# Expert down products taken in pairs in a fused attention and mixture-of-experts kernel: both heads, then all 48-row tails

## The reference

```
scores = softmax(x @ gate_w.T); topk_w, topk_idx = top_k(scores, 6); topk_w /= sum(topk_w)
buf[e, slot] = x[token]                     # at most C = 384 tokens per expert
g = buf @ w_gate[e].T; u = buf @ w_up[e].T  # 256 -> 176
eo = (silu(g) * u) @ w_down[e].T            # 176 -> 256
y[token] += eo[e, slot] * topk_w
return y + shared_swiglu(x)
```

## Time and profile before

| what | us |
|---|---|
| median of 3 runs | 542.45 (541.57 to 545.41) |
| span of the profiled execution | 581.2 |
| PE busy in it | 528.9 (91%) |
| DVE, ACT, POOL busy | 348.5, 301.3, 334.4 |

### The profile page before, as it was taken

How to read it: one execution, slowest core, us unless ns; L and a number is a source line. 1 busy time by engine, 2 the same in 40 slices (tenths; PEclk the granted TensorE clock), 3 DMA queues, 4 the chain that set the end, 5 groups by cost and what they waited for, 6 DMA issues and landing times.

```text
span 581.2 us, 13626 instructions
## 1 busy us (share of the span) xinstructions
PE 528.9 (91%) x4267; PEld 446.2 (77%) x4267; DVE 348.5 (60%) x1107; ACT 301.3 (52%) x899; POOL 334.4 (58%) x365
## 2 busy tenths in 40 slices
PE   8799998988989894969999999999988999999991
PEld 7698988888889883858877878787766787778681
DVE  4968877777777874756554555555454555455512
ACT  3797777778777863311234444455544444445410
POOL 4482254555444546575146766766666676678840
PEclk9898998889777976899999999999999999999997
DMA  9999997722222222122999999999989999977556
GB/s 292 388 373 394 404 390 280 228 84 84 73 74 74 83 74 88 57 98 78 321 267 300 252 245 230 236 244 251 251 217 231 241 238 233 231 143 115 73 116 140
DMA packets 65857, 119.01 MB, mean 205 GB/s; under 512 B 11216, under 2 KB 43280, under 8 KB 62704
## 3 DMA queue, kind: packets, MB, share of 16 engines
q0 software_dynamic: 24576, 56.39, 37.0%
q1 hardware_dynamic: 39584, 58.75, 33.2%
q10 hardware_dynamic: 1616, 2.90, 1.4%
HBM read 57.28 MB, written 60.23 MB: 202 GB/s over the span
## 4 chain that ended last, share of the span: by engine, by line
PE 75%; DVE 7%; issue 4%; another core or an unknown queue 4%; ACT 4%; POOL 2%; DMA 1%; ACTq 0%; DVEq 0%
PE PS L958 17%; PE PS L976 9%; PE PS L962 7%; PE PS L979 7%; PE PS L629 4%; PE PS L945 4%; PE PS L696 4%; PE PS L809 3%; PE PS L767 3%; PE PS L609 3%; PE PS L784 2%; PE PS L713 2%; PE PS L795 2%; PE PS L719 2%
## 5 line engine op out<-in xcount | busy, mean ns | idle before, releaser
L1836 POOL DMA_INDIRECT expert_rows<-XR,slot x96 | 95.1, 990 | 86.9 <-PE PS L629 58.7
L1859 POOL DMA_INDIRECT out<-YE,dest x64 | 93.6, 1462 | 45.2 <-issue 24.7
L1859 POOL DMA_INDIRECT acc_b<-YE,dest x64 | 93.7, 1465 | 37.4 <-issue 14.0
L1234 ACT ACTIVATE YE<-PS,wsel 104x256 f32<-104x256 f32 (+14 forms) x128 | 53.4, 467 | 96.5 <-PE PS L979 78.1
L1061 ACT ACTIVATE SMX<-SMX,smax 128x112 f32<-128x112 f32 x256 | 75.0, 392 | 0.2 <-DVE smax L1464 0.2
L1649 DVE TENSOR_TENSOR HE<-SL,PS 128x216 f32<-128x216 f32 (+12 forms) x64 | 23.2, 362 | 52.0 <-ACT SL L1221 39.5
L1070 ACT COPY PT<-PS 112x512 f32<-112x512 f32 x64 | 36.0, 595 | 21.0 <-remote 15.8
L767 PE MATMUL PS<-VW,PT 112*64 112x17 f32 x960 | 35.8, 213 | 11.2 <-issue 11.2
L1640 DVE COPY XET<-PS 128x432 f32<-128x432 f32 (+12 forms) x64 | 36.5, 572 | 15.6 <-PE PS L945 11.4
L1626 DVE SCALAR_TENSOR_TENSOR hit<-XG,by_rank 112x12 f32<-112x12 f32 (+3 forms) x64 | 14.6, 229 | 49.3 <-DMA out<-YE,dest 33.7
L767 PEld LDWEIGHTS PS<-VW,PT 112*64 112x64 f32 x960 | 32.6, 140 | 14.8 <-issue 12.7
(11 more groups left out here) (236 smaller groups left out, 1146.0 us busy)
## 6 DMA issues: line engine op xcount, KB each, us to landing
expert_rows<-zero POOLq DMA_DIRECT2D x24, 1088.0 KB, 14.0
W<-in_w SPq DMA_DIRECT2D x24, 368.0 KB
XG<-expert_rows SPq DMA_DIRECT2D x24, 238.0 KB
XB<-in_w SPq DMA_DIRECT2D x15, 368.0 KB
SMX<-in_w SPq DMA_DIRECT2D x15, 368.0 KB
XG<-expert_rows SPq DMA_DIRECT2D x24, 204.0 KB
W<-in_w SPq DMA_DIRECT2D x24, 128.0 KB
XG<-expert_rows SPq DMA_DIRECT2D x10, 272.0 KB
```

Of the source, the lines that this page charges most:

```text
L1234: act.mul(YE[0:h, e.slot, t, :], PS[0:h, 5 + t, e.odd * D:(e.odd + 1) * D], wsel[0:h, e.slot, t:t + 1]).then_inc(y_ready, 1)
L1836: pool.indirect_dma_start(rows, bass.IndirectOffsetOnAxis(ap=slot[:, d2 % UN, k:k + 1], axis=0), XR[:, d2 % UN, :], None, bounds_check=EX ...
L1859: pool.indirect_dma_start(target, bass.IndirectOffsetOnAxis(ap=dest[0:h, e.slot, t:t + 1], axis=0), YE[0:h, e.slot, t, :], None, bounds_ch ...
```

## The change

PE takes the downs of experts e and e + 1 together, when e + 1 has been reached: both heads, then both tails, into the two halves of the same PSUM banks (only the first head opens the bank). Hidden products go one expert further ahead (e + 2) and turned rows two further (e + 4). HE gets four slots, in the space of the attention's PT; YE six (YS), with six semaphores; wsel and dest twelve (AHEAD). SP issues weights 10 experts ahead of the rows' counter instead of 12, after the rows of p + 4.

```
...
+YS = 6
...
-        wsel = sb("wsel", [P, UN, 2])
+        wsel = sb("wsel", [P, AHEAD, 2])
...
-        dest = sb("dest", [P, UN, 2], I32)
+        dest = sb("dest", [P, AHEAD, 2], I32)
...
-        HE = sb("HE", [P, 2, 2, MAIN])
-        YE = sb("YE", [P, UN, 2, D])
+        HE = PT[:, :, :, :].rearrange("p g j q -> p (g j q)").rearrange("p (u t n) -> p u t n", u=UN, t=2)
+        YE = sb("YE", [P, YS, 2, D])
...
# SP
                     expert_rows(expert(n), n % UN, 0, 2, HALF[n])
                     if p < 2:
                         weights(expert(AHEAD - 2 + p), AHEAD - 2 + p)
-                    if p + AHEAD < EX:
-                        sp.wait_ge(dn_done, p + 1)
-                        weights(expert(p + AHEAD), p % AHEAD)
+                    elif p - 2 + AHEAD < EX:
+                        sp.wait_ge(dn_done, p - 1)
+                        weights(expert(p - 2 + AHEAD), (p - 2) % AHEAD)
...
# PE
+                def down_head(e, opens):
+                    j, h = home(e), half(e)
+                    c = slice(e.odd * D, (e.odd + 1) * D)
+                    for t in range(nt):
+                        pe.matmul(PS[0:h, 5 + t, c], HE[:, e.slot, 0, t * h:(t + 1) * h], W2S[j][:, 0, :],
+                                  start=opens, stop=False)
+                def down_tail(e, closes):
+                    j, h = home(e), half(e)
+                    c = slice(e.odd * D, (e.odd + 1) * D)
+                    for t in range(nt):
+                        r = slice(64 * t, 64 * t + FT)
+                        mm = pe.matmul(PS[0:h, 5 + t, c], HE[r, e.slot, 1, t * h:(t + 1) * h], W2S[j][r, 1, :],
+                                       start=False, stop=closes)
+                    mm.then_inc(dn_done, 1)
...
+                def down_two(e):
+                    pe.wait_ge(h_ready, e.times(2, 4))
+                    pe.wait_ge(w2_doubled, e.times(1, 2))
+                    if not e.first():
+                        pe.wait_ge(y_ready, sums_before(e, nt))
+                    down_head(e, True)
+                    down_head(e + 1, False)
+                    down_tail(e, False)
+                    down_tail(e + 1, True)
...
+                def step(e):
+                    if has(e + 2, end):
+                        hidden(e + 2)
+                    if has(e + 4, end):
+                        rows_t(e + 4)
+                    if e.odd:
+                        down_two(e - 1)
...
                 hidden(Step(0))
+                rows_t(Step(2))
                 pe.wait_ge(sh_add, NT - NTL)
+                hidden(Step(1))
+                rows_t(Step(3))
                 in_flight(pe, step, half is even_half)
...
# ACT
-                    act.wait_ge(dn_done, e.times(1, 1))
+                    act.wait_ge(dn_done, e.times(1, 2 - e.odd if nt == 2 else 1))
...
+                def step(e):
+                    if has(e + 2, end):
+                        silus(e + 2)
+                        doubled(e + 2)
+                    if e.odd:
+                        weighted(e - 1)
+                        weighted(e)
...
# DVE
-                    if not e.first(UN):
-                        dve.wait_ge(y_stored[j], adds_before(e, nt))
+                    if nt == 1:
+                        dve.wait_ge(y_stored[y_home(e)], adds_before(e, nt))
+                    elif not e.first(AHEAD):
+                        dve.wait_ge(y_stored[y_home(e)], e.turn(32, -32, YS))
...
-                    if not e.first(2):
-                        dve.wait_ge(dn_done, e.times(1, -1))
+                    if not e.first(UN):
+                        dve.wait_ge(dn_done, e.times(1, 1 - UN))
...
+                lead = nt
+                def ahead(e):
+                    if has(e, end):
+                        product(e)
+                    if has(e + lead, end):
+                        rows_t(e + lead)
+                    if has(e, end):
+                        tail_products(e)
+                        choices(e)
                 def step(e):
+                    ahead(e + nt)
...
# POOL
+                pool.memset(YE[:, UN:YS, :, :], 0.0)
...
-                    hold(pool, y_stored[before.slot], before.turn(32, 32))
+                    hold(pool, y_stored[y_home(before)], before.turn(32, 32, YS))
...
```

More of the change, by code:

```diff
@@ L418, in home, with y_home, y_uses @@
             return e.off % AHEAD
+        def y_home(e):
+            return e.off % YS
+        def y_uses(j, end=EX):
+            return (end - 1 - j) // YS + 1
         def adds_before(e, nt):
-            return e.turn(32) if nt == 2 else e.turn(16, 16 * EX // UN)
+            return e.turn(32, 0, YS) if nt == 2 else e.turn(16, 16 * y_uses(y_home(e)), YS)
         def sums_before(e, nt):
@@ L525, in _ @@
                         weights(expert(AHEAD - 2 + p), AHEAD - 2 + p)
-                    if p + AHEAD < EX:
-                        sp.wait_ge(dn_done, p + 1)
-                        weights(expert(p + AHEAD), p % AHEAD)
+                    elif p - 2 + AHEAD < EX:
+                        sp.wait_ge(dn_done, p - 1)
+                        weights(expert(p - 2 + AHEAD), (p - 2) % AHEAD)
             with sp.Else():
[L530 to L539, removed]
+                for p in range(2):
                     sp.wait_ge(et_done, p + 1)
@@ L542, in _ @@
                     expert_rows(expert(p + UN), p % UN, 0, 2)
-                    if p + AHEAD < EX:
-                        sp.wait_ge(dn_done, p + 1)
-                        weights(expert(p + AHEAD), p % AHEAD)
+                    weights(expert(AHEAD - 2 + p), AHEAD - 2 + p)
+                with sp.Fori(0, EX // AHEAD - 1) as i:
+                    for j in range(AHEAD):
+                        hold(sp, et_done, i * AHEAD + (j + 3))
+                        hold(sp, idx_ready, i * AHEAD + (j + 3))
+                        expert_rows(expert(i * AHEAD + (j + 2 + UN)), (j + 2) % UN, 0, 2)
+                        hold(sp, dn_done, i * AHEAD + (j + 1))
+                        weights(expert(i * AHEAD + (j + AHEAD)), j)
+                for p in range(EX - EX % AHEAD - AHEAD + 2, EX - UN):
+                    sp.wait_ge(et_done, p + 1)
+                    sp.wait_ge(idx_ready, p + 1)
+                    expert_rows(expert(p + UN), p % UN, 0, 2)
+                    if p - 2 + AHEAD < EX:
+                        sp.wait_ge(dn_done, p - 1)
+                        weights(expert(p - 2 + AHEAD), (p - 2) % AHEAD)
                 def rest(p, j):
@@ L964, in hidden, with step_one @@
                     mm.then_inc(gt_done, 1)
+                def down_head(e, opens):
[12 more added lines that the diff above has]
+                    mm.then_inc(dn_done, 1)
                 def down(e):
[L967 removed]
                     pe.wait_ge(h_ready, e.times(2, 2))
[L970 to L971 removed]
+                    pe.wait_ge(y_ready, sums_before(e, nt))
+                    down_head(e, True)
+                    down_tail(e, True)
+                def down_two(e):
+                    pe.wait_ge(h_ready, e.times(2, 4))
+                    pe.wait_ge(w2_doubled, e.times(1, 2))
                     if not e.first():
                         pe.wait_ge(y_ready, sums_before(e, nt))
[L974 to L983, removed]
+                    down_head(e, True)
+                    down_head(e + 1, False)
+                    down_tail(e, False)
+                    down_tail(e + 1, True)
+                def step_one(e):
                     if has(e + 1, end):
@@ L1246, in step @@
                     weighted(e)
-                    if nt == 2 and has(e + 2, end):
+                def step(e):
+                    if has(e + 2, end):
+                        silus(e + 2)
                         doubled(e + 2)
+                    if e.odd:
+                        weighted(e - 1)
+                        weighted(e)
                 if nt == 1:
                     silus(Step(EX))
-                    rest_in_flight(act, step)
+                    rest_in_flight(act, step_one)
                     return
@@ L1256, in experts @@
                 silus(Step(0))
+                silus(Step(1))
                 in_flight(act, step, half is even_half)
@@ L1677, in experts @@
                 product(first)
-                tail_products(first)
                 if nt == 1:
+                    tail_products(first)
                     rest_in_flight(dve, step)
                 else:
+                    rows_t(first + 2)
+                    tail_products(first)
+                    ahead(first + 1)
                     in_flight(dve, step, half is even_half)
@@ L1881, in rest @@
                 before = e - 1
-                hold(pool, y_stored[before.slot], before.turn(16, 16 * EX // UN + 16))
+                hold(pool, y_stored[y_home(before)], before.turn(16, 16 * y_uses(y_home(before)) + 16, YS))
                 added(e, acc_b, 1, P)
@@ L1889, in landed @@
             def landed(nt):
```

(5 more changed lines are left out.)

39 lines of the change are left out of this document (16 added, 23 removed).

## The result

Over four runs each, the changed kernel took 594.18 us (590.2 to 597.58) and the kernel before 543.93 (541.57 to 545.53): a ratio of 1.092, interval 1.086 to 1.098. It is slower by 50 us. The forecast was 568, the upper end of its range 592.

A forecast was written before the change was run, and what follows sets the result against it. PE's own work bound the kernel before; late odd rows on SP's queue would then set 9.1 us per pair. 26 turns, start, last pairs and adds add 27 us, 608 against 581.2, scaled to 568 us; range 544 to 592.

The forecast's parts named there:

- a loop through SP's queue and the odd rows: SP asks for odd rows only after the pair's wait and three weight issues, so PE waits; 555 to 583 us, 60%.
- The saving by pairs: On PE, one of two passages into and out of the down tails goes: 0.37 us per pair, 11.8 us over 32.
- the first rival: Rows are in time at L945 of odd experts and PE gains: loop 199.4 us, time 533 us, chance 10%.
- The pair's turn of 9.1 us: 0.32 + 2.22 + 3.2 landing + 0.3 restart + 0.3 turning + 2.77 down, at every size; 26 turns make 236.6 us.
- the lone rows: The last rows, issued alone at 536.29, had all 112 packets moved in 2.3 us; the lower bound for landing.
- an upper 4.35: Upper bound for the odd rows' landing after L477, with 544 KB of weights ahead of them in SP's queue, none moved.
- The start, the last pairs, the end: First pair start B at 305.9 from hidden 0 at 287.55; last pairs 34.1 us; last adds 3.1 us more.
- The ratio 608.2 / 581.2: Forecast span over the profiled span of before, 1.046, carried over to the median run of 542.45: 568 us.
- the adds' loop at 8.6 us per pair: Adds to `out`: expert e waits until e - 2 has landed, a turn of 8.6 us that no ring shortens.
- the second rival: Short landing, nothing moves: rows land in 2.3 us, a pair takes 8.2; 546 us, chance 17%.
- The weights clog the queue: Third rival: rows land at the upper 4.35 us behind the weights, a pair takes 10.25; 598 us, chance 13%.
- The rings: Longer rings ease DVE's and ACT's waits; they return at most PE's 5.8 us of idle in the loop.

The follow-up runs named there:

- second profile of before: The kernel before, unchanged, run again for another profile; run time 542.14 us, span 540.4.
- xg6: The changed kernel with six buffers for gathered rows instead of four, silu's tile moved into the dead query tile; 547.24 us, ratio 1.011.
- thin: The changed kernel, loading only 64 columns of each part of the weights issued between the even and odd rank's rows; 589.46 us, ratio 1.086.
- rings_only: The kernel before with only the longer rings (six YE slots, twelve of wsel and dest), no pairs or new order; 542.2 us, ratio 1.001.

## Why the prediction was right and wrong

**Which way, and by what: right.** The kernel became slower by a loop through SP's queue and the odd rows, the bound that the forecast put at 60%. The chain above is its sum written out by the profile. Its signs are all there: PE idle before L957 once in two experts (mostly 0.5 to 1.5 us at 108 rows and more, 1.8 to 2.2 at 84); pairs of 9.0 to 9.9 at full clock, but for one of 10.55 whose rows took 4.6 from issue to use, with no trend from 128 rows (9.03) to the smallest experts (9.12); L486 at 2.6 us behind the pair's first product; a gap of 0.36 on each side of eight tails; DVE's waits for adds gone (39.8 us in the second profile of before); DMA share 0.84.

**The saving by pairs: right.** 0.37 per pair was forecast. Three pairs at 96 rows without late rows took 7.56, 7.56 and 7.54, where two experts before took 7.90: 0.35. With rows in time (`xg6`) the middle took 199.5; the first rival had worked out 199.4.

**The pair's turn of 9.1 us: the step that failed.** Its terms at full clock, over the 19 pairs that waited: rows issued at 2.73 (2.54 forecast), from issue to turning 3.52 (3.5: 3.2 landing and 0.3 restart), turning 0.39 (0.3), down 2.87 (2.77): 9.51. Each is a little long, and the disputed one, the landing, came out right. That was luck in part: 3.2 was chosen between the lone rows' 2.3 and an upper 4.35 that counted the bytes ahead in full, and `thin` gives the 436 KB of them that it leaves out at most 0.6. With the first pair, 20 pairs took 189.7 in all: 7.7 us over the forecast. The six others took 11.26, 2.16 more than forecast: 13.0 us. There the mis-sized term is the paired down, 4.48 instead of 2.77, because the durations of PE's work in the turn came from 300 to 420 us of before, where PE was never idle and its clock at 1.00. The forecast put idle into PE's loop and went on pricing PE's work at the clock of a loop without it. Together they are the middle's excess over 236.6, 20.7 of the 26 us that were missing.

**The start, the last pairs, the end.** From hidden 0 to hidden 4 the forecast had 18.4 us and the profile 19.4; for the last pairs both have 34.1. The end was to grow by 3.1; it grew by 3.4 against the first profile of before (31.9 against 28.5), by 4.1 against the second.

**The ratio 608.2 / 581.2: wrong, and cheap.** The forecast scaled its 27 us down because the profiled execution was long. The length sat in a stretch that the change does not touch, so the 27 us belonged whole on top of 542.45: 569.5 instead of 568. Its loop was 2 us longer than that of the second profile as well.

**The rivals.** "The rows are in time" was to give 533. `xg6` put them in time and gave 547. The sum for PE was right, but that rival carried PE's gain through to the end, though the forecast had the adds' loop at 8.6 us per pair and only compared it with 9.1. Against PE's pairs in `xg6`, 6.7 to 8.2 from the sixth on, it is the longer one; the forecast said so beside the second rival, and not where it decided. "The weights clog the queue" came nearest in time (598), but not by its reason: the landing was 3.5 with restart, not 4.65.

**The rings: right in kind.** The 4 to 6 us of PE's waits were all that they could return, and in `rings_only` 1.9 of the 4.3 came back at the end, with no change of the time that can be told from noise.

## What to carry to other kernels

When a change makes work ready later in a loop of several engines, follow what releases what all the way round and sum that ring; here the sum through SP's queue held nearly term by term, and PE's hidden products, a part of the bound until then, had left it. Then ask what the new idle does to the durations taken from the old trace: PE, idle for 18% of a stretch, did not keep the clock that they were measured at. And before an engine's gain is carried to the end, set every other loop's turn beside the new one, not beside the old.

## What the runs showed that was not expected

- PE's granted clock fell behind waits of 1.81 to 2.81 us in an otherwise full loop: six pairs, 0.84 to 0.87 over the pair, a paired down of 4.48 us instead of 2.87. It did not fall each time: waits of 2.05, 2.20 and 2.21 us left it at 1.00. With dummies in the wait (0.0 to 1.4 us of idle left) it never fell.
- Gathered rows still took 2.88 us from issue to use with some 100 KB of weights ahead of them, against 3.52 behind 544 KB.
- One execution of the kernel before had a front of 287 us, a second one 249; the nine other profiles lay between 250 and 256. PEclk over the front was 0.89 in the long one and 0.96 in the second; what made it so stays open.
